# Moving three pieces of work in the first batch of a quantised residual adapter stack, and the rounding of x2 in every batch

## The chip, the cores and the metric

The kernel runs on one core of one Trainium2 chip. The time is the device time of one launch in microseconds (us): 489.69 us, the median of three runs that lay between 489.37 and 489.79. Lower is better. Four engines compute side by side, each with its own program in its own order: TensorE (PE), VectorE (DVE), ScalarE (ACT) and GpSimd (POOL). SyncE (SP) issues the DMAs. They are tied together by semaphores alone.

## The reference, cut to what matters

The input x has 8 batches of 256 tokens of 1024 features. Four residual layers follow each other:

```python
# layer 0: 8 thresholds pick one (delta, zero point) pair for each element
gi  = sum(|x| <= thresholds);  idx = min(gi, 7)
d, zp = deltas[idx], zero_points[idx]
q   = (clip(round(x / d) + zp, 0, 63) - zp) * d
x   = x + where(gi == 8, 0, q)
# layer 1: one 1024x1024 weight per batch, out of 8
x   = x + x @ W1[adapter[b]].T
# layer 2: a shared 1024x1024 weight and a rank-32 adapter
x   = x + x @ W2.T + 0.5 * (x @ lora_A[labeler[b]]) @ lora_B.T
# layer 3: a rank-16 adapter
x   = x + (x @ B3[adapter[b]].T) @ A3[adapter[b]].T
```

All in float32. In the kernel layers 2 and 3 become one product x2 (I + W2)^T and one low-rank product of rank 48: small tables G and E, computed once at the start, fold the adapter of layer 3 over the result of layer 2.

## The kernel before, in words

**Units and steps.** The 256 tokens of a batch are two units of 128 tokens, so there are 16 units. Unit c takes eight steps on ACT and DVE, one for each threshold group; a step is numbered n, and step n belongs to unit n // 8. In step n ACT does `multiple(n)` (L329: x / d plus a rounding constant, into tq) and `exceeds(n-2)` (L344: the mask |x| > threshold), DVE does `value(n)` (L439), `clamp(n-1)` (L448) and `select(n-2)` (L460, a predicated copy under the mask). After the last step of a unit DVE's `close_unit` (L466, L448, L473) writes x1 of that unit; ACT's absx (L337) follows for the next one. ACT and DVE both run this loop written out in full, each with its other duties attached to fixed steps by a table of numbers: with s = n - 16 b, the rounding of x2 (`round_x2` on ACT, L353, to x2h) and its remainder (`split_x2` on DVE, L479, to x2l) stood at s = 13 and 15 for the first unit of a batch and at 21 and 23 for the second one (`X2_AT`), the rounding of the low-rank factor U at 19, 20 (ACT) and 21 (DVE), that of V at 14 and 15.

**PE in one batch.** `w1_x1(b, 0)` is 64 float32 products (128 records, L598) that write x2 of the first unit into two banks of 4 tiles; each bank is released to ACT when its 4 tiles are done. Then `product(0, k)` for k = 0 to 7 (L620): x2h times w2h, x2h times w2l, x2l times w2h, each in two halves of 512 columns; k = 0 to 3 need the first half of x2l, k = 4 to 7 the second. Then PE waits for x1 of the second unit, does `w1_x1(b, 1)`, the low-rank `v_x2` (L611) and `product(1, k)`, and goes over to the next batch. The last low-rank step of batch b (`u_low`, L630 and L632) is done inside `w1_x1(b+1, 0)`, after three tiles.

**The first batch.** It also prepares the tables. PE computes D (`bilinear`, L562) and G (`adapters_g`, L572, L574). ACT copies G out (L394), and SP stores it to DRAM and reads a slice back for each batch. `adapters_e` (L586, L587) makes E into four banks; ACT copies it to outb (L404), SP stores it. W2 comes in eight pieces of 512 KB through four staging buffers, three in `ring` and one in `ua`; POOL adds the identity on the diagonal (L290), ACT rounds a piece (L400, to w2h), DVE takes the remainder (L511, to w2l), and the buffer is free for the piece four further on. `ua` is also where U lands, so U of batch 0 may be loaded only when the last piece that used `ua` is split. Before, ACT did the eight pieces in steps 9 to 16, DVE in steps 10 to 17, one a step; PE waited for w2l of piece k before `product(0, k)`.

SP issues in the order of its program; a wait in it holds all that is behind. In a batch it loads V, x of the second unit of the next batch, the first quarter of W1 of the next batch, then waits until U is split (`ul_ready`), loads U, and then the other three quarters of W1.

Of the kernel before, what the change touches and what calls it, by code (L numbers as in the profile page):

```python
# [5 lines left out]
def quantised_residual_adapter_stack(nc, x, params, w1, w2t, w2n, b3t, b2n, b2r, a3, la, ids_b, ids_a,  # L6
# [13 lines left out]
    B, _, UN, KT, _ = x.shape  # L20
    T = UN * P
    OT = KT
    G = params.shape[2]
# [6 lines left out]
    HALF = KT // 2  # L30
# [15 lines left out]
    with ctx:  # L46
# [47 lines left out]
        stage = [ring[:, i, :] for i in range(ST - 1)] + [ua[:, :]]  # L94
# [78 lines left out]
        def _(sp):  # L173
# [69 lines left out]
            sp.wait_ge(w2l_ready, KT)  # L243
# [64 lines left out]
        DVE_D, ACT_G = 5, 9  # L308
        ACT_E = (15, 15, 16, 16)
        ACT_W2, DVE_W2 = 9, 10  # L310

        X2_AT = (13, 15)

        ACT_V, DVE_V = 14, 15
        ACT_U, DVE_U = 19, 21
# [6 lines left out]
        def _(act):  # L322
# [67 lines left out]
            def tables(n):  # L390
# [6 lines left out]
                if ACT_W2 <= n < ACT_W2 + KT:  # L397
                    k = n - ACT_W2
                    act.wait_ge(w2_diag, k + 1)
                    nc.scalar.activation(w2h[:, k, :], stage[k % ST], ACT.Copy).then_inc(w2h_ready, 1)  # L400
# [8 lines left out]
            for n in range(END):  # L409
# [4 lines left out]
                for i in range(2):  # L414
                    c, off = divmod(n - X2_AT[i], G)
                    if off == 0 and 0 <= c < UN * B:
                        round_x2(c, i)
# [17 lines left out]
        def _(dve):  # L435
# [64 lines left out]
            def tables(n):  # L500
# [7 lines left out]
                if DVE_W2 <= n < DVE_W2 + KT:  # L508
                    k = n - DVE_W2
                    dve.wait_ge(w2h_ready, k + 1)  # L510
                    nc.vector.tensor_tensor(w2l[:, k, :], stage[k % ST], w2h[:, k, :].bitcast(f32),  # L511
                                            ALU.subtract).then_inc(w2l_ready, 1)
# [14 lines left out]
            for n in range(END):  # L527
# [18 lines left out]
                for i in range(2):  # L546
                    c, off = divmod(n - X2_AT[i], G)
                    if off == 0 and 0 <= c < UN * B:
                        split_x2(c, i)
# [7 lines left out]
        def _(pe):  # L557
# [59 lines left out]
            def product(t, k, halves=(0, 1)):  # L617
                for xs, w in ((x2h, w2h), (x2h, w2l), (x2l, w2h)):
# [18 lines left out]
            def batch(b, first=False, last=False):  # L637
                pe.wait_ge(x1_ready, UN * b + 1)
                if first:
                    w1_x1(b, 0, range(OT))  # L640
                    adapters_e()
# [5 lines left out]
                for k in range(KT):  # L647
                    if k % HALF == 0:
                        pe.wait_ge(x2l_ready, BANKS * b + k // HALF + 1)
                    if first:  # L650
                        if k == 0:
                            pe.wait_ge(g_ready, 2)
                        pe.wait_ge(w2l_ready, k + 1)
                    elif k == 0:
                        pe.wait_ge(out_ready, ACCS * (b - 1) + 2)
                    product(0, k)
                pe.wait_ge(x1_ready, UN * b + 2)
                if first:
                    pe.wait_ge(e_ready, 2 * EH)
                w1_x1(b, 1, range(OT))  # L660
# [10 lines left out]
                if last:  # L671
                    for h in range(2):
                        for k in range(early, KT):
                            product(1, k, (h,))
# [9 lines left out]
            adapters_g()  # L684
            batch(0, first=True)
# [53 lines left out]
```

## Time and profile before

| what | value |
|---|---|
| median of three runs | 489.69 us |
| the profiled execution, its own time | 490.88 us |
| its span | 489.1 us |
| PE busy | 467.4 us, 96% of the span |
| DVE busy | 416.3 us, 85% |
| ACT busy | 355.2 us, 73% |

All rows below come from the one profiled execution, whose own time is 1.8 us more than its span. A row of the timeline gives the start (us from the span's start), how long, the engine, the line, the operation, out <- in, the number of instructions, and in brackets how long the engine had been idle before it and what released it. The records of one engine overlap a little (the next one starts before the end of the last is recorded), so the price of an operation in a sequence is best read from start to start. The heavy parts of PE are seen as groups of 128 records of L598, once for each unit.

### The profile page before, as it was taken

What the parts mean: (1) busy time and instruction counts of PE and PEld (TensorE: products, weight loads), DVE (VectorE), ACT (ScalarE), POOL (GpSimd) and SP (SyncE); (2) the same over time, 40 slices, a digit from 0 to 9 for tenths busy, and PEclk for the clock granted to TensorE, in tenths of its full rate; (3) what the DMA queues carried; (4) which work ended last, traced back from release to release, by engine and by line L of the source; (5) the groups of instructions that cost most, each with busy time, mean ns of one, the idle gap of its engine ahead of it and who ended that gap; (6) DMA issues with size and microseconds to landing.
All of it is one profiled execution on the core that took longest, in us unless ns stands there. A gap on an engine that the chain in (4) does not pass through costs nothing.

```text
span 489.1 us, 8214 instructions
## 1 busy us (share of the span) xinstructions
PE 467.4 (96%) x3184; PEld 427.3 (87%) x3184; DVE 416.3 (85%) x480; ACT 355.2 (73%) x384; POOL 52.7 (11%) x46
## 2 busy tenths in 40 slices
PE   3959989999999999999999999999999999999997
PEld 3959669899898979899898979899898979899995
DVE  4999989988999789978999799978999799979310
ACT  6968589759878588759878588759878588758011
POOL 1064100400012001300022000300022001200000
PEclk9998999999999999999999999999999999999999
DMA  7997136612381116512381116512381116502002
GB/s 277 412 373 261 44 119 193 244 44 85 100 325 56 43 59 203 216 43 81 109 306 67 44 59 208 211 43 84 112 302 66 43 60 208 210 2 86 1 1 86
DMA packets 17830, 67.07 MB, mean 137 GB/s; under 512 B 2576, under 2 KB 5904, under 8 KB 13712
## 3 DMA queue, kind: packets, MB, share of 16 engines
q1 hardware_dynamic: 17808, 66.81, 38.1%
q8 instruction: 10, 0.16, 0.1%
q14 instruction: 12, 0.10, 0.1%
HBM read 56.84 MB, written 9.96 MB: 137 GB/s over the span
## 4 chain that ended last, share of the span: by engine, by line
PE 75%; DVE 12%; ACT 9%; issue 2%; DMA 1%; DVEq 0%; SPq 0%; ACTq 0%
PE x_bank L598 48%; PE acc L620 20%; ACT tq L329 4%; DVE y L460 4%; PE x_bank L611 3%; ACT mask L344 3%; DVE uq L466 2%; DVE x L473 2%; PE acc L632 2%; PE acc L630 2%; ACT outb L388 1%; DVE tq L439 1%; DVE y L448 1%; DVE uq L448 1%; DMA xin<-x 1%
## 5 line engine op out<-in xcount | busy, mean ns | idle before, releaser
L598 PEld LDWEIGHTS x_bank<-x,w1b 128*128 128x128 f32 x2048 | 234.2, 194 | 14.8 <-DVE x L473 13.5
L598 PE MATMUL x_bank<-x,w1b 128*128 128x128 f32 x2048 | 235.9, 277 | 10.4 <-DVE x L473 10.4
L329 ACT ACTIVATE tq<-xin,magic,rdelta 128x1024 f32<-128x1024 f32 x128 | 157.1, 1236 | 3.3 <-DMA xin<-x 3.1
L460 DVE COPY_PREDICATED y<-mask,uq 128x1024 f32<-128x1024 int16 x112 | 150.8, 1346 | 0.1
L344 ACT ACTIVATE mask<-absx,negtop 128x1024 bf16<-128x1024 f32 x112 | 127.8, 1141 | 6.2 <-DVE y L460 5.7
L439 DVE TENSOR_SCALAR tq<-tq,par 128x1024 f32<-128x1024 f32 x128 | 98.4, 769 | 11.6 <-ACT tq L329 5.4
L448 DVE TENSOR_SCALAR uq<-tq,ylow,yhigh 128x1024 f32<-128x1024 f32 x112 | 91.8, 820 | 3.3 <-issue 1.7
L295 POOL TENSOR_TENSOR w1b<-w1b,eye 128x256 f32<-128x256 f32 x32 | 42.0, 1312 | 364.5 <-DMA w1b<-w 364.5
L620 PE MATMUL acc<-w2h,x2h 128*128 128x512 f32 x256 | 81.1, 394 | 0.0
L620 PE MATMUL acc<-w2l,x2h 128*128 128x512 f32 x256 | 80.1, 390 | 0.0
L620 PE MATMUL acc<-w2h,x2l 128*128 128x512 f32 x256 | 79.9, 389 | 0.0
L353 ACT ACTIVATE x2h<-x_bank 128x512 fp32r<-128x512 f32 x32 | 19.1, 597 | 80.8 <-PE x_bank L598 80.8
L620 PEld LDWEIGHTS acc<-w2l,x2h 128*128 128x128 f32 x256 | 48.1, 188 | 10.2
L620 PEld LDWEIGHTS acc<-w2h,x2l 128*128 128x128 f32 x256 | 48.1, 188 | 10.2
L479 DVE TENSOR_TENSOR x2l<-x_bank,x2h 128x512 fp32r<-128x512 f32 x32 | 22.0, 689 | 37.8 <-ACT x2h L353 37.0
L620 PEld LDWEIGHTS acc<-w2h,x2h 128*128 128x128 f32 x256 | 46.5, 188 | 8.8 <-DVE x2l L479 0.2
L337 ACT ACTIVATE absx<-xin 128x1024 f32<-128x1024 f32 x16 | 16.9, 1056 | 9.3 <-DVE uq L466 9.3
L388 ACT ACTIVATE outb<-acc 128x512 f32<-128x512 f32 x32 | 18.0, 593 | 7.5 <-PE acc L632 7.5
L466 DVE SCALAR_TENSOR_TENSOR uq<-absx,top,y 128x1024 f32<-128x1024 f32 x16 | 22.9, 1432 | 0.6
L473 DVE TENSOR_TENSOR x<-xin,uq 128x1024 f32<-128x1024 f32 x16 | 20.0, 1252 | 0.0
L574 PE MATMUL acc<-x,w1b 128*128 128x128 f32 x128 | 18.0, 301 | 0.0
L574 PEld LDWEIGHTS acc<-x,w1b 128*128 128x128 f32 x128 | 17.4, 218 | 0.0
(56 smaller groups left out, 217.1 us busy)
## 6 DMA issues: line engine op xcount, KB each, us to landing
w1b<-w SPq DMA_DIRECT2D x32, 1024.0 KB, 6.5
xin<-x SPq DMA_DIRECT2D x16, 512.0 KB, 3.7
out<-outb SPq DMA_DIRECT2D x14, 512.0 KB, 2.7
w1b<-w2n SPq DMA_DIRECT2D x4, 1024.0 KB, 10.1
ring<-w2t SPq DMA_DIRECT2D x6, 512.0 KB, 7.3
ua<-e_dram SPq DMA_DIRECT2D x16, 128.0 KB, 2.5
ua<-w2t SPq DMA_DIRECT2D x2, 512.0 KB, 6.1
va<-la SPq DMA_DIRECT2D x8, 128.0 KB, 2.7
```

Of the source, the lines that this page charges most:

```text
L295: nc.gpsimd.tensor_tensor(diag, diag, eye[:, :].unsqueeze(1).to_broadcast([P, 2, P]), ALU.add) \
L329: nc.scalar.activation(tq[:, n % TQ, :], flat(xin, c % UN), ACT.Identity, bias=magic[:, 0:1], scale=rdelta[:, g:g + 1]).then_inc(t_ready, 1)
L344: nc.scalar.activation(mask[:, n % MK, :], absx[:, :], ACT.Relu, bias=negtop[:, g:g + 1], scale=1.0).then_inc(mask_ready, 1)
L388: nc.scalar.activation(outb[:, t, h * DH:(h + 1) * DH], acc[q][:, :], ACT.Copy).then_inc(out_ready, 1)
L439: nc.vector.tensor_scalar(tq[:, n % TQ, :], tq[:, n % TQ, :], -MAGIC, par[:, 1, g:g + 1], ALU.add, ALU.mult).then_inc(u_ready, 1)
L448: nc.vector.tensor_scalar(clamped_y, tq[:, n % TQ, :], ylow[:, g:g + 1], yhigh[:, g:g + 1], ALU.max, ALU.min).then_inc(clamped, 1)
L460: nc.vector.copy_predicated(y[:, :], mask[:, n % MK, :].bitcast(i16), uq[:, n % 2, :]) \
L466: nc.vector.scalar_tensor_tensor(ycut, absx[:, :], top[:, G - 1:G], y[:, :], ALU.is_gt, ALU.mult).then_inc(y_cut, 1)
L473: nc.vector.tensor_tensor(flat(x1, c % UN), flat(xin, c % UN), ycut, ALU.add).then_inc(x1_ready, 1)
L574: last = nc.tensor.matmul(into, w2g[:, i, o * P:(o + 1) * P], b3s[:, o, :], start=False, stop=(o == OT - 1))
L598: last = nc.tensor.matmul(x2_bank[2 * t + i][:, o % HALF * P:(o % HALF + 1) * P], w1b[:, o, at:at + P], x1[:, t, k, :], start=(o % HALF == ...
L620: nc.tensor.matmul(acc[2 * t + h][:, :], xs[:, t, k, :], w[:, k, h * DH:(h + 1) * DH], start=(k == 0 and xs is x2h and w is w2h), stop=Fal ...
```

## The change

1. `adapters_e` is called behind `adapters_g`, ahead of the first batch, and no longer between `w1_x1(0, 0)` and the first product. ACT's copies of E go from steps 15, 15, 16, 16 to 12, 13, 13, 14.
2. ACT rounds x2 at s = 14 and 16 (and 22 and 24), a step further on than before; DVE's remainder stays at 13 and 15 (21 and 23). ACT and DVE run in step only through their semaphores, so ACT may be ahead of DVE by a step or more.
3. In the first batch the product of the first unit is cut: the two parts with w2h for all eight k, then the part with w2l for k = 0 to 3, then `w1_x1(0, 1)`, and then the part with w2l for k = 4 to 7. PE waits for w2h of a piece at the first, for w2l at the second and third. DVE splits pieces 0 to 3 in steps 10 to 13 as before, and pieces 4 to 7 in steps 18 to 21.
4. The four staging buffers are renamed: `ua` holds pieces 0 and 4 in place of 3 and 7, and SP loads U of batch 0 when five pieces are split instead of eight.
5. The rounding of U is two steps later in every batch (ACT 21 and 22, DVE 23), ACT's copy of G one step later (10).

```diff
-        stage = [ring[:, i, :] for i in range(ST - 1)] + [ua[:, :]]
+        stage = [ua[:, :]] + [ring[:, i, :] for i in range(ST - 1)]
...
-            sp.wait_ge(w2l_ready, KT)
+            sp.wait_ge(w2l_ready, ST + 1)
             load_u(a0)
...
-        DVE_D, ACT_G = 5, 9
-        ACT_E = (15, 15, 16, 16)
-        ACT_W2, DVE_W2 = 9, 10
-
-        X2_AT = (13, 15)
+        DVE_D, ACT_G = 5, 10
+        ACT_E = (12, 13, 13, 14)
+        ACT_W2, DVE_W2 = (9, 10, 11, 12, 13, 14, 15, 16), (10, 11, 12, 13, 18, 19, 20, 21)
+
+        ACT_X2, DVE_X2 = (14, 16), (13, 15)
...
-        ACT_U, DVE_U = 19, 21
+        ACT_U, DVE_U = 21, 23
...
-            def product(t, k, halves=(0, 1)):
-                for xs, w in ((x2h, w2h), (x2h, w2l), (x2l, w2h)):
+            HIGH, LOW = ((x2h, w2h), (x2l, w2h)), ((x2h, w2l),)
+            ALL = (HIGH[0], LOW[0], HIGH[1])
+
+            def product(t, k, parts=ALL, halves=(0, 1)):
+                for xs, w in parts:
...
                 if first:
                     w1_x1(b, 0, range(OT))
-                    adapters_e()
...
-                        pe.wait_ge(w2l_ready, k + 1)
+                        pe.wait_ge(w2h_ready, k + 1)
...
-                    product(0, k)
+                    product(0, k, HIGH if first else ALL)
+                if first:
+                    for k in range(HALF):
+                        pe.wait_ge(w2l_ready, k + 1)
+                        product(0, k, LOW)
+                    pe.wait_ge(e_ready, 2 * EH)
                 pe.wait_ge(x1_ready, UN * b + 2)
+                w1_x1(b, 1, range(OT))
                 if first:
-                    pe.wait_ge(e_ready, 2 * EH)
-                w1_x1(b, 1, range(OT))
+                    for k in range(HALF, KT):
+                        pe.wait_ge(w2l_ready, k + 1)
+                        product(0, k, LOW)
...
             bilinear()
             adapters_g()
+            adapters_e()
             batch(0, first=True)
```

**PE, the start of the first batch.** acc and x2_bank are the banks of PSUM, outb holds the inputs of E. Before:

```order
L574 MATMUL acc1<-x1,w1b 128x128 x8
L598 MATMUL x2_bank0<-x1,w1b 128x128 x32
L598 MATMUL x2_bank1<-x1,w1b 128x128 x32
L586 MATMUL acc2<-outb,eye 128x512
L587 MATMUL acc2<-outb,dmask 128x512
L586 MATMUL acc3<-outb,eye 128x512
L587 MATMUL acc3<-outb,dmask 128x512
L586 MATMUL x2_bank2<-outb,eye 128x512
L587 MATMUL x2_bank2<-outb,dmask 128x512
L586 MATMUL x2_bank3<-outb,eye 128x512
L587 MATMUL x2_bank3<-outb,dmask 128x512
L620 MATMUL acc0<-w2h,x2h 128x512
```

The same place in the changed kernel:

```order
L574 MATMUL acc1<-x1,w1b 128x128 x8
L586 MATMUL acc2<-outb,eye 128x512
L587 MATMUL acc2<-outb,dmask 128x512
L586 MATMUL acc3<-outb,eye 128x512
L587 MATMUL acc3<-outb,dmask 128x512
L586 MATMUL x2_bank2<-outb,eye 128x512
L587 MATMUL x2_bank2<-outb,dmask 128x512
L586 MATMUL x2_bank3<-outb,eye 128x512
L587 MATMUL x2_bank3<-outb,dmask 128x512
L598 MATMUL x2_bank0<-x1,w1b 128x128 x32
L598 MATMUL x2_bank1<-x1,w1b 128x128 x32
L623 MATMUL acc0<-w2h,x2h 128x512
```

The eight products of E moved from behind the W1 product to ahead of it; the line of the W2 product is L623 in the changed kernel.

**DVE, the first batch, from the second remainder of x2 to x1 of the second unit.** L479 is the remainder of x2, L511 that of a piece of W2, L473 writes x1. Before:

```order
L479 TENSOR_TENSOR x2l<-x_bank,x2h 128x512
L460 COPY_PREDICATED y<-mask,uq 128x1024
L511 TENSOR_TENSOR w2l<-ring,w2h 128x1024
L439 TENSOR_SCALAR tq<-tq,par 128x1024
L448 TENSOR_SCALAR uq<-tq,ylow,yhigh 128x1024
L460 COPY_PREDICATED y<-mask,uq 128x1024
L511 TENSOR_TENSOR w2l<-ua,w2h 128x1024
L439 TENSOR_SCALAR tq<-tq,par 128x1024
L460 COPY_PREDICATED y<-mask,uq 128x1024
L466 SCALAR_TENSOR_TENSOR uq<-absx,top,y 128x1024
L448 TENSOR_SCALAR y<-tq,ylow,yhigh 128x1024
L473 TENSOR_TENSOR x<-xin,uq 128x1024
```

The same stretch in the changed kernel:

```order
L479 TENSOR_TENSOR x2l<-x_bank,x2h 128x512
L460 COPY_PREDICATED y<-mask,uq 128x1024
L439 TENSOR_SCALAR tq<-tq,par 128x1024
L448 TENSOR_SCALAR uq<-tq,ylow,yhigh 128x1024
L460 COPY_PREDICATED y<-mask,uq 128x1024
L439 TENSOR_SCALAR tq<-tq,par 128x1024
L460 COPY_PREDICATED y<-mask,uq 128x1024
L466 SCALAR_TENSOR_TENSOR uq<-absx,top,y 128x1024
L448 TENSOR_SCALAR y<-tq,ylow,yhigh 128x1024
L473 TENSOR_TENSOR x<-xin,uq 128x1024
L511 TENSOR_TENSOR w2l<-ua,w2h 128x1024
```

The remainders of W2 left this stretch and stand behind L473 (two more left the stretch just before it).

**ACT, a later batch, around the rounding of x2 of the first unit.** L353 is the rounding, from x2_bank0 and x2_bank1; L388 copies the result of the batch before. Before:

```order
L344 ACTIVATE mask<-absx,negtop 128x1024
L353 ACTIVATE x2h<-x2_bank0 128x512
L329 ACTIVATE tq<-xin,magic,rdelta 128x1024
L344 ACTIVATE mask<-absx,negtop 128x1024
L388 ACTIVATE outb<-acc0 128x512
L388 ACTIVATE outb<-acc1 128x512
L362 ACTIVATE v_hl<-va 128x8x32
L363 ACTIVATE v_hl<-vg 128x8x16
L329 ACTIVATE tq<-xin,magic,rdelta 128x1024
L344 ACTIVATE mask<-absx,negtop 128x1024
L353 ACTIVATE x2h<-x2_bank1 128x512
L388 ACTIVATE outb<-acc2 128x512
```

The same place in the changed kernel:

```order
L344 ACTIVATE mask<-absx,negtop 128x1024
L353 ACTIVATE x2h<-x2_bank0 128x512
L388 ACTIVATE outb<-acc0 128x512
L388 ACTIVATE outb<-acc1 128x512
L362 ACTIVATE v_hl<-va 128x8x32
L363 ACTIVATE v_hl<-vg 128x8x16
L329 ACTIVATE tq<-xin,magic,rdelta 128x1024
L344 ACTIVATE mask<-absx,negtop 128x1024
L388 ACTIVATE outb<-acc2 128x512
L329 ACTIVATE tq<-xin,magic,rdelta 128x1024
L344 ACTIVATE mask<-absx,negtop 128x1024
L353 ACTIVATE x2h<-x2_bank1 128x512
```

Each rounding now has one more pair of L329 and L344 ahead of it and one fewer behind it.

## Rows read from the trace of the kernel before

**Rows 1.** The page, part 1: busy time of each engine (share of the span), instructions.

```profile
PE 467.4 (96%) x3184; PEld 427.3 (87%) x3184; DVE 416.3 (85%) x480; ACT 355.2 (73%) x384; POOL 52.7 (11%) x46
```

**Rows 2.** Waits of PE: who waited for whom, us in total, times, longest.

```profile
PE x_bank L598 <- DVE x L473: 10.4, 8, 5.0
```

**Rows 3.** Timeline of PE, first batch.

```profile
35.64 17.21 PE L598 MATMUL x_bank<-x,w1b 128*128 128x128 f32 x128 [5.02 <-DVE x L473]
52.69 1.02 PE L586 MATMUL acc<-outb,eye 128*128 128x512 f32 x2
...
72.60 14.56 PE L598 MATMUL x_bank<-x,w1b 128*128 128x128 f32 x128 [1.95 <-DVE x L473]
...
99.79 5.52 PE L598 MATMUL x_bank<-x,w1b 128*128 128x128 f32 x48
```

**Rows 4.** Windows of PE: stretch, length, busy (count), granted clock, DMA share, GB/s.

```profile
34.00:35.00 1.00, 0.00 (x0) 0.71 1.08 352
```

**Rows 5.** Timeline of PE, later batches.

```profile
181.69 0.61 PE L620 MATMUL acc<-w2h,x2l 128*128 128x512 f32 x2
182.80 14.56 PE L598 MATMUL x_bank<-x,w1b 128*128 128x128 f32 x128 [0.50 <-DVE x L473]
...
209.99 5.52 PE L598 MATMUL x_bank<-x,w1b 128*128 128x128 f32 x48
...
456.78 14.45 PE L598 MATMUL x_bank<-x,w1b 128*128 128x128 f32 x128
```

**Rows 6.** Timeline of DVE, the second and third batch.

```profile
122.50 0.75 DVE L439 TENSOR_SCALAR tq<-tq,par 128x1024 f32<-128x1024 f32 x1 [0.91 <-ACT mask L344]
...
172.06 0.69 DVE L479 TENSOR_TENSOR x2l<-x_bank,x2h 128x512 fp32r<-128x512 f32 x1 [0.47 <-ACT x2h L353]
...
174.77 0.81 DVE L448 TENSOR_SCALAR uq<-tq,ylow,yhigh 128x1024 f32<-128x1024 f32 x1
...
177.42 0.75 DVE L439 TENSOR_SCALAR tq<-tq,par 128x1024 f32<-128x1024 f32 x1 [0.56 <-ACT mask L344]
...
181.53 1.22 DVE L473 TENSOR_TENSOR x<-xin,uq 128x1024 f32<-128x1024 f32 x1
...
192.07 0.68 DVE L479 TENSOR_TENSOR x2l<-x_bank,x2h 128x512 fp32r<-128x512 f32 x1
...
202.82 0.91 DVE L439 TENSOR_SCALAR tq<-tq,par 128x1024 f32<-128x1024 f32 x1 [0.20 <-DVE y L460]
...
207.43 1.22 DVE L473 TENSOR_TENSOR x<-xin,uq 128x1024 f32<-128x1024 f32 x1
```

**Rows 7.** Timeline of ACT, the third batch.

```profile
164.28 0.60 ACT L353 ACTIVATE x2h<-x_bank 128x512 fp32r<-128x512 f32 x1 [4.98 <-PE x_bank L598]
164.77 1.23 ACT L329 ACTIVATE tq<-xin,magic,rdelta 128x1024 f32<-128x1024 f32 x1
165.91 1.14 ACT L344 ACTIVATE mask<-absx,negtop 128x1024 bf16<-128x1024 f32 x1
...
171.43 0.60 ACT L353 ACTIVATE x2h<-x_bank 128x512 fp32r<-128x512 f32 x1 [0.74 <-PE x_bank L598]
...
190.25 0.60 ACT L353 ACTIVATE x2h<-x_bank 128x512 fp32r<-128x512 f32 x1 [0.96 <-PE x_bank L598]
```

**Rows 8.** Timeline of DVE, first batch.

```profile
51.32 1.20 DVE L511 TENSOR_TENSOR w2l<-ring,w2h 128x1024 fp32r<-128x1024 f32 x1
...
58.27 0.68 DVE L479 TENSOR_TENSOR x2l<-x_bank,x2h 128x512 fp32r<-128x512 f32 x1
...
71.32 1.22 DVE L473 TENSOR_TENSOR x<-xin,uq 128x1024 f32<-128x1024 f32 x1
...
97.94 1.22 DVE L473 TENSOR_TENSOR x<-xin,uq 128x1024 f32<-128x1024 f32 x1
```

**Rows 9.** Timeline of ACT, first batch.

```profile
41.04 1.04 ACT L400 ACTIVATE w2h<-ua 128x1024 fp32r<-128x1024 f32 x1
```

**Rows 10.** The page, part 6: DMA issues, KB each, us from issue to landing.

```profile
w1b<-w SPq DMA_DIRECT2D x32, 1024.0 KB, 6.5
```

More of the change, by code:

```diff
@@ L396, in tables @@
                                              ACT.Copy).then_inc(g_ready, 1)
-                if ACT_W2 <= n < ACT_W2 + KT:
-                    k = n - ACT_W2
+                if n in ACT_W2:
+                    k = ACT_W2.index(n)
                     act.wait_ge(w2_diag, k + 1)
@@ L414, in _ @@
                 for i in range(2):
-                    c, off = divmod(n - X2_AT[i], G)
+                    c, off = divmod(n - ACT_X2[i], G)
                     if off == 0 and 0 <= c < UN * B:
@@ L507, in tables @@
                         .then_inc(dmask_ready, 1)
-                if DVE_W2 <= n < DVE_W2 + KT:
-                    k = n - DVE_W2
+                if n in DVE_W2:
+                    k = DVE_W2.index(n)
                     dve.wait_ge(w2h_ready, k + 1)
@@ L546, in _ @@
                 for i in range(2):
-                    c, off = divmod(n - X2_AT[i], G)
+                    c, off = divmod(n - DVE_X2[i], G)
                     if off == 0 and 0 <= c < UN * B:
@@ L673, in batch @@
                         for k in range(early, KT):
-                            product(1, k, (h,))
+                            product(1, k, ALL, (h,))
                         if h == 0:
```

## The prediction, made before the changed kernel ran

> **What bounds the kernel now.** The page comes first: PE is busy for 96% of the span [rows 1]. So the time is PE's work plus the little that PE waits. The waits of PE are the second view: nearly all that belongs to the batches is one kind, the W1 product waits for x1 from DVE, eight times, 10.4 us [rows 2]. PE's timeline splits the sum: 5.02 and 1.95 us in the first batch [rows 3], five waits of 0.50 in the third to seventh [rows 5], which leaves 0.9 for the second; the last batch has none. A W1 product behind a wait is recorded with 14.56 us, the one that did not wait (at 456.78) with 14.45, so a wait also costs a start-up of 0.11 [rows 5].
>
> Two more costs are in these rows. The first W1 product took 17.21 us instead of 14.56 [rows 3], because PE had stood still for 5.02 us and the granted clock had fallen from 2.4 towards 1.2 GHz near 34.5 us [rows 4]: 2.65 us. And PE's wait for the x1 of a second unit is DVE's chain from the second remainder of x2 to L473. In the third batch DVE is held twice there by ACT: L439 idles 0.56 us for a mask at 177.42, and L448 at 174.77 starts some 0.2 late for the mask before it [rows 6].
>
> **The steady part: rounding a step later.** ACT idles 4.98 us before it rounds the first bank of x2 [rows 7], waiting for PE, and only afterwards does the L329 and L344 that DVE will want. With the rounding behind them that pair (1.14 + 1.03 = 2.17 us, the second being 1.14 less an overlap of 0.1 [rows 7]) falls into the idle time. ACT from 164.28 is then: rounding 0.49, two result copies 0.97, V 0.5, pair 2.17, a result copy 0.49, pair 2.17, which is 171.07. PE gives the second bank for rounding at 171.43 [rows 7]. So ACT gets there 0.36 us early, the second rounding is not late, and DVE's L479 stays at 172.06 [rows 6]. The copy and V prices are estimates from the 0.49 of an equal or larger tile.
>
> Behind it ACT needs 0.49 + 0.49 + 2.17 for the mask that held DVE: 174.6, or about 175.1 if the mask waits for the predicated copy two steps back. DVE wants it at about 176.9. Both holds go. What stays of the 0.56 is 0.20, the time DVE needs for its own copy's signal at a unit's end, as at 202.82 [rows 6]. DVE gains 0.36 + 0.20 = 0.56 per batch. PE's gap is from the last product, 181.69 + 0.45 = 182.14, to 182.80, that is 0.66 [rows 5], so 0.10 of it stays and the start-up too. Five batches: 5 x 0.56 = 2.8. In the second batch the hold was 0.91 [rows 6]: 0.71 + 0.20 = 0.91, of a PE gap of about 1.05. Sum of the steady part 3.7 us.
>
> The bounds of this term: nothing, if DVE remains held; 5 x (0.66 + 0.11) + 1.05 + 0.11 = 5.0 us if PE never waits again. I take 3.7 since each piece of it is in a row.
>
> **What the later step costs elsewhere.** For a second unit DVE's first remainder was not held: 192.07, no idle [rows 6]. ACT rounded at 190.25, after a wait of 0.96 for PE [rows 7]. Now a pair of 2.17 and one more U rounding order stand ahead; U itself (two pieces of 0.95) has moved back, so ACT reaches the rounding at about 190.25 - 0.96 - 0.95 + 2.17 + some waiting for DVE's copy = 190.5 to 191.0. It ends near 191.5. DVE no longer has the 1.25 us of the U remainder ahead and arrives at 192.07 - 1.25 = 190.8. It waits 0.7 to 0.8, ends up 0.5 us ahead of before, and then pays the U remainder two steps on: 0.7 late. x1 of the next first unit was ready at 207.43 + 1.22 = 208.65, and PE wanted it at 209.99 [rows 5, 6]: slack 1.34, of which 0.7 is used. Cost nothing. SP holds three quarters of W1 until U is split, now some 6.6 us later (two steps of 2.6 and a remainder). They land 6.5 us after the issue [rows 10], near 206 to 210; PE wants the second quarter two tiles (3.6 us) behind 209.99. Cost nothing, and 3 us later it would begin to cost.
>
> **The first batch.** E is eight times 0.86 us (1.02 recorded for a pair of records, 0.16 of it overlap [rows 3]): 6.9. It stood between 52.8 and 59.7, on PE's path. G ends at 35.64 - 5.02 = 30.6. E fills 30.6 to 37.5, in the old wait, and the clock has no reason to fall. The W1 product starts 1.9 later, at 37.5, and takes 14.5: it ends at 52.0 instead of 52.8. PE is then 7.7 us earlier at the W2 product. That gain can't pass: PE next needs x1 of the second unit, which comes from DVE.
>
> DVE is the same up to its first remainder of x2 near 49.5. ACT sets the second: piece 3 of W2 is rounded at 41.04, when POOL gives it [rows 9], and until the second rounding of x2 stand four W2 pieces (4 x 0.95 = 3.8; 1.04 recorded less overlap), four pairs (8.7), four copies of E and the first rounding (5 x 0.49 = 2.45), V 0.5 and about 0.3 for POOL's next diagonal: 15.7, so it starts at 56.7. DVE's second remainder follows 0.63 later, as 172.06 follows 171.43 [rows 6, 7]: 57.3 instead of 58.27 [rows 8]. From there to L473 it is now exactly the sequence of a later batch, whose 181.53 - 172.06 = 9.47 less the 0.56 held gives 8.91: L473 starts at 66.2 instead of 71.32 [rows 8], 5.1 us sooner. Two pieces of W2 and 1.9 us of being held left this stretch. x1 is ready at 67.45 and PE, which has waited since about 63.5 (a part of the W2 product also waits, near 55.6 to 58), starts `w1_x1(0, 1)` at 67.5 and not at 72.60.
>
> PE then works as before, 99.79 - 72.60 = 27.19 us, plus the eight products with w2l that were put behind (4 x 0.45 = 1.8). It is done at 96.5. But DVE pays for the four W2 pieces now: from L473 to the next L473 26.62 us before, and 4 x 1.13 more (1.20 less overlap [rows 8]) is 31.1. The next L473 starts at 97.3, x1 is ready at 98.55, PE starts at 98.6. Before it was 99.79 without a wait. The gain is 99.79 - 98.6 - 0.11 = 1.1 us. **That is what remains of the 5.1:** PE waits 2.1 us in a new place. Bounds: nothing, if DVE loses one more microsecond on this path; 99.79 - 96.5 = 3.3 if it loses none to the four pieces.
>
> **Sum.** 1.1 + 3.7 = 4.8. The profiled execution had 490.88, so 486.1 for its like; the median of the runs stands 1.19 lower, and I apply the difference to it: 489.69 - 4.8 = 484.9 us.
>
> **The rivals.**
> A. The clock falls in the new wait. PE stands still from 63.5 to 67.5, 4.0 us. 1.95 us did not lower the clock (the product behind it took 14.56), 5.02 did [rows 3], at about 3.9 us from its start [rows 4]. Price: the next W1 product 2.65 longer, PE done at 99.1 instead of 96.5, x1 long there at 98.6. The slack of 2.1 hides most of it: 0.5 us, so 485.4.
> The Trainium skill, in TensorE: Matmul & The Clock Gate, under HAM oscillation, warns that a pause of PE between bursts can put the clock at half so that the next burst starts slow. By that rule this rival would be the likely case; the trace agrees for 5.02 us and shows the contrary for 1.95.
>
> B. The steady part gives nothing: DVE is held by something else in the same stretch (its own signals, ACT late after all since the early margin is only 0.36). For it: PE's gap of 0.66 is small and DVE is busy 85% [rows 1]. Against it: both holds name the mask. 489.69 - 1.1 = 488.6.
>
> C. Slower. x1 of the first unit of each next batch comes late, because DVE's first remainder of a second unit now waits for an ACT that runs a further step ahead. Its slack is 1.34, I use 0.7. If ACT arrives one more pair late (2.17), PE waits 2.17 - 0.64 + 0.11 = 1.6 in six transitions: 9.8 us lost, 489.69 - 4.8 + 9.8 = 494.7. It turns slower than before when ACT is more than 1.4 us later than worked out. Against it: ACT idled 0.96 there [rows 7], and its busy share is 73% [rows 1].
>
> D. DVE's chain gains more than I count, and PE never waits in the steady part and hardly at 98.6: 489.69 - 5.0 - 2.2 = 482.5.
>
> **Chances.** My forecast 0.55, A 0.18, B 0.12, C 0.06, D 0.09. The likeliest one's own range is 484.2 to 485.8. The range of 8 in 10 takes in A and most of D and goes part of the way to B: 483.0 to 487.4. A measurement of this kernel tells 0.2%, about 1 us, from no change. B sits on that line, half of it counts as the same. Faster 0.88, same 0.06, slower 0.06.
>
> **What would show it.** E stands at 30.6 to 37.5 and the granted clock stays at 2.4 GHz up to 52. x1 of the second unit near 67.4, and PE waits about 4 us for it, then about 2 us for the next one near 98.6. In later batches L439 at a second unit's end is released by DVE's own copy after 0.20, and PE's waits fall from 0.50 to 0.1 or less. ACT's second rounding still idles for PE. It would be wrong if DVE's L479 waited more than 1 us for the rounding of a second unit, if the waits of 0.50 stayed, or if PE waited for W1's second quarter.

## The result, and the profile after

The changed kernel took 486.01 us (median of 5 runs, 484.91 to 486.41) where the kernel before took 489.69 (489.16 to 490.94). The ratio is 0.9919 with the interval 0.9903 to 0.9935: 3.7 us faster, forecast 4.8 (484.9, range 483.0 to 487.4). The profiled execution had 486.40 us and a span of 484.6, so 4.48 less than its counterpart before. The rows below place all of this 4.48. The medians differ by only 3.68: the profiled execution of the kernel before was 1.19 us above its median, that of the changed kernel 0.39 above its own. So 0.80 of the 4.48 lies in which executions were profiled, and the rows can't say where in the kernel before.

The page, part 1, of the changed kernel. It answers to [rows 1].

```profile
PE 465.8 (96%) x3184; PEld 426.1 (88%) x3184; DVE 418.6 (86%) x480; ACT 359.5 (74%) x384; POOL 45.2 (9%) x46
```

PE's work is the same within 0.4%, and PE is still the bound. Waits of the changed kernel, the lines on PE and two on ACT: who waited for whom, us in total, times, longest. The first line, ahead of the rest, is from the kernel before.

```profile
ACT mask L344 <- DVE y L460: 5.7, 9, 0.8
```

```profile
ACT mask L344 <- DVE y L460: 40.1, 48, 2.5
...
ACT x2h L353 <- PE x_bank L598: 28.7, 16, 13.4
...
PE x_bank L598 <- DVE x L473: 4.0, 2, 3.7
...
PE acc L623 <- DVE x2l L479: 3.3, 1, 3.3
```

The 10.4 us in eight waits for x1 [rows 2] are 4.0 in two, and one wait for the second remainder of x2 is new. ACT now waits for DVE's copies before its masks, 40.1 us where it was 5.7: it has run ahead, which is what removes DVE's holds. Timeline of PE, changed kernel, the answer to [rows 3, 5]:

```profile
29.45 1.02 PE L586 MATMUL acc<-outb,eye 128*128 128x512 f32 x2
...
36.31 14.45 PE L598 MATMUL x_bank<-x,w1b 128*128 128x128 f32 x128
...
57.68 0.73 PE L623 MATMUL acc<-w2h,x2h 128*128 128x512 f32 x2 [3.27 <-DVE x2l L479]
...
61.44 1.98 PE L623 MATMUL acc<-w2l,x2h 128*128 128x512 f32 x8
67.16 17.30 PE L598 MATMUL x_bank<-x,w1b 128*128 128x128 f32 x128 [3.75 <-DVE x L473]
84.22 2.09 PE L623 MATMUL acc<-w2l,x2h 128*128 128x512 f32 x8
...
98.96 5.52 PE L598 MATMUL x_bank<-x,w1b 128*128 128x128 f32 x48
...
126.46 14.56 PE L598 MATMUL x_bank<-x,w1b 128*128 128x128 f32 x128 [0.28 <-DVE x L473]
153.65 5.52 PE L598 MATMUL x_bank<-x,w1b 128*128 128x128 f32 x48
...
180.26 0.61 PE L623 MATMUL acc<-w2h,x2l 128*128 128x512 f32 x2
180.74 14.56 PE L598 MATMUL x_bank<-x,w1b 128*128 128x128 f32 x128
...
207.96 5.52 PE L598 MATMUL x_bank<-x,w1b 128*128 128x128 f32 x48
...
425.24 5.52 PE L598 MATMUL x_bank<-x,w1b 128*128 128x128 f32 x48
```

Three things are to be seen. E stands at 29.45, in the old wait, and the first W1 product has its full speed. The second W1 product starts 5.4 us earlier than before, yet takes 17.30 us, and the second batch (98.96, before 99.79) starts only **0.83 us** earlier. From there to the last batch's first product are 425.24 - 98.96 = 326.28 us, before 429.72 - 99.79 = 329.93: **3.65 us** less in six periods. 0.83 + 3.65 = 4.48, the whole difference of the spans.

Windows of PE, changed kernel (columns as in [rows 4]):

```profile
66.00:67.00 1.00, 0.00 (x0) 0.58 0.00 0
...
72.00:73.00 1.00, 1.00 (x6) 0.51 0.00 0
73.00:74.00 1.00, 1.00 (x11) 1.00 0.00 0
```

The granted clock fell from 2.4 to 1.2 GHz near 66.2, while PE stood still for x1, and came back at 73.0. Six products in a microsecond become eleven: the same work at half the clock. Timeline of DVE, changed kernel, the answer to [rows 6, 8]:

```profile
56.93 0.69 DVE L479 TENSOR_TENSOR x2l<-x_bank,x2h 128x512 fp32r<-128x512 f32 x1 [0.52 <-ACT x2h L353]
...
65.80 1.22 DVE L473 TENSOR_TENSOR x<-xin,uq 128x1024 f32<-128x1024 f32 x1
...
96.52 1.21 DVE L473 TENSOR_TENSOR x<-xin,uq 128x1024 f32<-128x1024 f32 x1
...
121.11 0.75 DVE L439 TENSOR_SCALAR tq<-tq,par 128x1024 f32<-128x1024 f32 x1 [0.57 <-DVE y L460]
...
170.62 0.69 DVE L479 TENSOR_TENSOR x2l<-x_bank,x2h 128x512 fp32r<-128x512 f32 x1 [0.71 <-ACT x2h L353]
...
175.41 0.75 DVE L439 TENSOR_SCALAR tq<-tq,par 128x1024 f32<-128x1024 f32 x1 [0.20 <-DVE y L460]
...
179.47 1.22 DVE L473 TENSOR_TENSOR x<-xin,uq 128x1024 f32<-128x1024 f32 x1
...
189.52 0.69 DVE L479 TENSOR_TENSOR x2l<-x_bank,x2h 128x512 fp32r<-128x512 f32 x1 [0.86 <-ACT x2h L353]
...
206.19 1.21 DVE L473 TENSOR_TENSOR x<-xin,uq 128x1024 f32<-128x1024 f32 x1
```

In the third batch L439 is held 0.20 by DVE's own copy, and no longer 0.56 by ACT's mask. In the second batch 0.57 of the 0.91 stays. Timeline of ACT, changed kernel, the answer to [rows 7]:

```profile
56.31 0.59 ACT L353 ACTIVATE x2h<-x_bank 128x512 fp32r<-128x512 f32 x1
...
162.84 0.60 ACT L353 ACTIVATE x2h<-x_bank 128x512 fp32r<-128x512 f32 x1 [0.93 <-PE x_bank L598]
...
169.99 0.60 ACT L353 ACTIVATE x2h<-x_bank 128x512 fp32r<-128x512 f32 x1 [0.25 <-PE x_bank L598]
```

The wait of 4.98 before the first rounding is 0.93. The pair of L329 and L344 (2.17) fills about half of the difference; most of the rest has turned into waits for DVE's copies ahead of the masks (0.64 us before, 1.56 + 0.36 now, between 150 us and the rounding). The second rounding still idles 0.25 for PE, so it is not late.

### The profile page after: what moved, and what is told of

Read it like the earlier page. It is cut to its first block, busy times and chain, and to the rows that moved or that the text cites. A ratio compares the mean times of both kernels' runs of the same rounds, so it can differ in the third digit from the quotient of the medians.

```text
span 484.6 us, 8214 instructions
## 1 busy us (share of the span) xinstructions
PE 465.8 (96%) x3184; PEld 426.1 (88%) x3184; DVE 418.6 (86%) x480; ACT 359.5 (74%) x384; POOL 45.2 (9%) x46
## 4 chain that ended last, share of the span: by engine, by line
PE 83%; DVE 8%; ACT 4%; DMA 2%; issue 1%; POOL 0%; DVEq 0%; SPq 0%; ACTq 0%
PE x_bank L598 45%; PE acc L623 32%; DVE y L460 4%; PE x_bank L611 3%; PE acc L635 2%; PE acc L633 2%; DVE uq L448 1%; ACT tq L329 1%; DMA ua<-w2t 1%; DMA xin<-x 1%; DVE x L473 1%; DVE uq L466 1%; ACT mask L344 1%; DVE tq L439 1%; ACT w2h L400 1%
## 5 line engine op out<-in xcount | busy, mean ns | idle before, releaser
L329 ACT ACTIVATE tq<-xin,magic,rdelta 128x1024 f32<-128x1024 f32 x128 | 157.0, 1234 | 3.7 <-DMA xin<-x 3.4
L344 ACT ACTIVATE mask<-absx,negtop 128x1024 bf16<-128x1024 f32 x112 | 128.5, 1147 | 40.8 <-DVE y L460 40.1
L439 DVE TENSOR_SCALAR tq<-tq,par 128x1024 f32<-128x1024 f32 x128 | 98.5, 769 | 8.5 <-ACT tq L329 4.8
L623 PE MATMUL acc<-w2h,x2h 128*128 128x512 f32 x256 | 80.9, 393 | 3.3 <-DVE x2l L479 3.3
L623 PE MATMUL acc<-w2h,x2l 128*128 128x512 f32 x256 | 79.9, 389 | 0.0
L623 PE MATMUL acc<-w2l,x2h 128*128 128x512 f32 x256 | 79.1, 390 | 0.0
L295 POOL TENSOR_TENSOR w1b<-w1b,eye 128x256 f32<-128x256 f32 x32 | 34.6, 1083 | 370.9 <-DMA w1b<-w 370.9
L623 PEld LDWEIGHTS acc<-w2h,x2l 128*128 128x128 f32 x256 | 48.1, 188 | 10.2
L623 PEld LDWEIGHTS acc<-w2l,x2h 128*128 128x128 f32 x256 | 48.0, 188 | 10.2
L623 PEld LDWEIGHTS acc<-w2h,x2h 128*128 128x128 f32 x256 | 46.3, 188 | 11.9 <-DVE x2l L479 3.7
L479 DVE TENSOR_TENSOR x2l<-x_bank,x2h 128x512 fp32r<-128x512 f32 x32 | 22.1, 689 | 36.2 <-ACT x2h L353 36.2
L353 ACT ACTIVATE x2h<-x_bank 128x512 fp32r<-128x512 f32 x32 | 19.0, 592 | 29.1 <-PE x_bank L598 28.7
L388 ACT ACTIVATE outb<-acc 128x512 f32<-128x512 f32 x32 | 18.1, 598 | 7.5 <-PE acc L635 7.5
L473 DVE TENSOR_TENSOR x<-xin,uq 128x1024 f32<-128x1024 f32 x16 | 20.0, 1249 | 0.0
L574 PE MATMUL acc<-x,w1b 128*128 128x128 f32 x128 | 16.9, 289 | 0.0
L611 PE MATMUL x_bank<-x2h,v_hl 128*128 128x256 f32 x64 | 16.3, 290 | 0.0
```

The costliest lines, as they stand in the source:

```text
L295: nc.gpsimd.tensor_tensor(diag, diag, eye[:, :].unsqueeze(1).to_broadcast([P, 2, P]), ALU.add) \
L329: nc.scalar.activation(tq[:, n % TQ, :], flat(xin, c % UN), ACT.Identity, bias=magic[:, 0:1], scale=rdelta[:, g:g + 1]).then_inc(t_ready, 1)
L344: nc.scalar.activation(mask[:, n % MK, :], absx[:, :], ACT.Relu, bias=negtop[:, g:g + 1], scale=1.0).then_inc(mask_ready, 1)
L439: nc.vector.tensor_scalar(tq[:, n % TQ, :], tq[:, n % TQ, :], -MAGIC, par[:, 1, g:g + 1], ALU.add, ALU.mult).then_inc(u_ready, 1)
L473: nc.vector.tensor_tensor(flat(x1, c % UN), flat(xin, c % UN), ycut, ALU.add).then_inc(x1_ready, 1)
L479: nc.vector.tensor_tensor(x2l[:, t, tiles, :].rearrange("p k t -> p (k t)"), x2_bank[2 * t + i][:, :], x2h[:, t, tiles, :].rearrange("p k ...
```

## The experiments

Two profile figures are given for most kernels: **start** is the start of the second batch's first W1 product (before 99.79, changed 98.96), **six** is the time from it to the last batch's (before 329.93, changed 326.28). The kernel before ran beside each: median 489.88 us beside the first four, 490.41 beside the next four, 489.46 beside the last four. One profile has one start, and starts of one kernel can differ by a microsecond or two, in part since W2's pieces come at other times; a claim on the first batch therefore wants a median as well.

**Only the rounding a step later**, on the kernel before.

```diff
-        X2_AT = (13, 15)
+        ACT_X2, DVE_X2 = (14, 16), (13, 15)
```

> The kernel before with ACT's rounding of x2 at 14 and 16 and nothing else. Main theory (ACT held DVE through the masks): the first batch is as before (W1 product of the second batch starts near 99.8 us), the periods between first units fall from 54.93 to about 54.3 and in the second batch from 55.30 to 54.7: 489.7 - 3.6 = 486.1 us. Rival (the steady gain of the changed kernel needs U two steps later too, because U ahead of the rounding of the second unit holds DVE): x1 of first units late, periods 54.6 or more, 487.5 or more.

Measured: 491.09 us, ratio 1.0029 (1.0015 to 1.0043), slower. six 326.38: the steady gain is whole. start 102.98: the first batch lost 3.2 us, which I had not expected. Timeline of ACT, this kernel:

```profile
58.53 1.09 ACT L404 ACTIVATE outb<-acc 128x512 f32<-128x512 f32 x2 [5.42 <-PE x_bank L587]
...
61.67 0.59 ACT L353 ACTIVATE x2h<-x_bank 128x512 fp32r<-128x512 f32 x1
```

ACT's copies of E stand in step 15. The second rounding, moved to 16, is now behind them, and PE has E done only at 58.5. DVE waits 4.38 us for it (L479 at 62.30), and x1 comes at 73.13 + 1.22. The other part is the clock. PE in this kernel:

```profile
74.41 15.92 PE L598 MATMUL x_bank<-x,w1b 128*128 128x128 f32 x128 [3.55 <-DVE x L473]
```

x1 is 1.81 later than before (L473 at 71.32 there), and behind the longer wait (3.55 for 1.95) the W1 product takes 1.36 more: 1.81 + 1.36 = 3.17 of the 3.19. So the later rounding wants E's copies out of its way.

**The rounding and U's later step**, on the kernel before.

```diff
-        X2_AT = (13, 15)
+        ACT_X2, DVE_X2 = (14, 16), (13, 15)
-        ACT_U, DVE_U = 19, 21
+        ACT_U, DVE_U = 21, 23
```

> As the one before, and U two steps later on ACT and DVE (21 and 22, 23). Main theory: the steady part of the changed kernel whole, 486.1 us, periods 54.3 as there. Rival (U matters): 1 us or more faster than the kernel with the rounding alone. Second rival (three quarters of W1 later cost something): slower than the rounding alone.

Measured: 491.19 us, 1.0025 (1.0009 to 1.0042); six 326.48, start 103.93. Against the run before it U's step is worth nothing in the steady part.

**Only the first batch's part**: the changed kernel with rounding and U on their old steps.

```diff
-        ACT_X2, DVE_X2 = (14, 16), (13, 15)
+        ACT_X2, DVE_X2 = (13, 15), (13, 15)
-        ACT_U, DVE_U = 21, 23
+        ACT_U, DVE_U = 19, 21
```

> The changed kernel with the rounding of x2 back at 13 and 15 and U back at 19 and 21: E behind G, the cut of the W2 product and the staging remain. Main theory: periods as before the change (54.93, 55.30), the W1 product of the second batch near 98.9 where the clock falls in PE's wait in the first batch and near 97.9 where it does not: 488.9 or 487.9 us. Rival (the rounding a step later is what makes the first batch quicker): the W1 product of the second batch starts at 99.8 or later, 489.7.

Measured: 490.94 us, 1.0011 (0.9994 to 1.0028). six 330.04 shows that the steady gain is the rounding's alone. start 100.77, where a gain was expected. Timeline of ACT, this kernel:

```profile
74.14 1.06 ACT L370 ACTIVATE u_hh<-ua 128x1024 fp32r<-128x1024 f32 x1 [5.56 <-DMA ua<-a]
```

The `ua` tile now holds W2's fifth piece, so SP loads U only when DVE has taken that remainder, behind L473: it starts at 68.21 here, the loads of U go out from 69.6 on, and ACT wants U in step 19, at 68.6. U's later step is thus not idle: it covers this load. The last experiment tests that. This profile is of one of the longer executions (491.97; they lie between 488.54 and 492.12), and W2's fifth piece held ACT 2.41 us in it.

**E behind G alone**, on the kernel before.

```diff
-        ACT_E = (15, 15, 16, 16)
+        ACT_E = (12, 13, 13, 14)
...
-                    adapters_e()
...
+            adapters_e()
```

> The kernel before with E behind G and ACT's copies of E at 12, 13, 13, 14, nothing else. DVE keeps four remainders of W2 ahead of x1 of the second unit; ACT no longer stands still for E. Main theory: DVE loses its 1.7 us of being held there, x1 of the second unit ready near 70.8 instead of 72.5; PE waits for it about 4 us, so the clock may fall: start of the second batch's W1 product 98.0 with the clock kept (488.0 us), 100.7 with the clock lost (490.6 us). Rival (moving E gives PE its 7 us back): 484 or less.

Measured: 489.61 us, 0.9998 (0.9986 to 1.001): nothing. Timeline of PE, this kernel:

```profile
37.52 14.45 PE L598 MATMUL x_bank<-x,w1b 128*128 128x128 f32 x128
...
70.11 17.05 PE L598 MATMUL x_bank<-x,w1b 128*128 128x128 f32 x128 [3.54 <-DVE x L473]
...
99.81 5.52 PE L598 MATMUL x_bank<-x,w1b 128*128 128x128 f32 x48
```

E took 6.9 us off PE's path, and none of it reached 99.8: PE waits for x1, the clock falls in that wait, and the W1 product gives back 2.5 (17.05 for 14.56), just what its earlier start had won (70.11 for 72.60). In one of the twelve executions the mean granted clock was 1.00: that one took 488.41 us, the shortest of all, and the one with the lowest clock (0.989) 491.58.

**The changed kernel without the cut of the W2 product.**

```diff
-        ACT_W2, DVE_W2 = (9, 10, 11, 12, 13, 14, 15, 16), (10, 11, 12, 13, 18, 19, 20, 21)
+        ACT_W2, DVE_W2 = (9, 10, 11, 12, 13, 14, 15, 16), (10, 11, 12, 13, 14, 15, 16, 17)
...
-                    product(0, k, HIGH if first else ALL)
+                    product(0, k)
-                if first:
-                    for k in range(HALF):
-                        pe.wait_ge(w2l_ready, k + 1)
-                        product(0, k, LOW)
...
-                if first:
-                    for k in range(HALF, KT):
-                        pe.wait_ge(w2l_ready, k + 1)
-                        product(0, k, LOW)
```

> The changed kernel with the W2 product of the first unit whole again and DVE's remainders of W2 in steps 10 to 17, one a step; E, staging, rounding and U as changed. Main theory: DVE meets all eight remainders ahead of x1 of the second unit, as before, which is ready near 71 us; the same work is only moved from behind L473 to ahead of it, so x1 of the next batch's first unit is ready at the same time, near 98, and PE, which then has less to do between, is ready at about 71 + 27.2 = 98.2 with the clock kept and 100.9 with it lost. So the cut is worth 0 to 2 us in the first batch: 485 to 488 us. Rival (the cut is what makes the first batch quicker): 3 us or more slower than the changed kernel.

Measured: 486.88 us, 0.9936 (0.9912 to 0.996); six 326.41, start 99.34. L473 is at 69.16 and the next at 97.37, where the changed kernel has 65.80 and 96.52. The cut brings x1 3.4 us forward and the next x1 0.85, and 0.4 at the start of the second batch. The W1 product between them took 16.16 here and 17.30 there, so part of what the cut brings goes to the clock. The interval overlaps the changed kernel's: in time, the cut's gain is not shown.

**Twelve more products before the wait for x1** (their result is overwritten), to hold the clock.

```diff
+                    for _ in range(12):
+                        nc.tensor.matmul(acc[2][:, :], x2h[:, 0, 0, :], w2h[:, 0, 0:DH], start=True, stop=False,
+                                         skip_group_check=True)
```

> The changed kernel with 12 idle products of 512 columns (2.7 us) into a free bank of the second unit at the start of PE's wait for x1 of the second unit; their results are overwritten. Main theory (the clock fell in that wait and made the W1 product 17.3 us instead of 14.5): clock at 1.00 all through, product 14.5 us, PE ready 2.8 us sooner for the second batch, but x1 of its first unit comes at 97.7, so only 1.1 us of it arrive: 1.1 us faster than the changed kernel where the clock had fallen (486.4 to 485.3), nothing where it had not. Rival (the product was long for another reason, DMA or POOL): no change. Rival (the clock's cost was whole on the path): 2.7 us faster, 483.7.

Measured: 484.90 us, 0.9895 (0.9871 to 0.992). six 326.55. Timeline and windows of PE, this kernel:

```profile
57.60 1.03 PE L623 MATMUL acc<-w2h,x2h 128*128 128x512 f32 x2 [2.45 <-DVE x2l L479]
...
64.76 2.88 PE L665 MATMUL acc<-w2h,x2h 128*128 128x512 f32 x12
67.48 14.45 PE L598 MATMUL x_bank<-x,w1b 128*128 128x128 f32 x128
...
97.77 5.62 PE L598 MATMUL x_bank<-x,w1b 128*128 128x128 f32 x48 [1.20 <-DVE x L473]
```

```profile
57.00:58.00 1.00, 0.40 (x2) 0.92 0.00 0
58.00:59.00 1.00, 1.00 (x4) 0.50 0.00 0
...
61.00:62.00 1.00, 1.00 (x5) 0.87 0.00 0
```

The W1 product is back at 14.45, and now PE waits for x1 at 97.77. Of the 2.85 saved 1.2 arrive, the rest is hidden by that x1. This second wait is the one that I had forecast. But the clock did not hold all through, as I had expected: in this execution it fell at 57.8, behind a pause of only 2.45 us, and came back at 61.3. The W2 product ended later for it, and the wait that the twelve products filled was about 2.2 us and not 3.75. The profile alone therefore does not show that they kept the clock. Better evidence are the six executions: their mean granted clock is 1.00 once and 0.999 twice (484.75, 484.86 and 484.92 us), and in none of the eleven executions of the changed kernel is it above 0.996. The interval of the ratio overlaps the changed kernel's.

**DVE's second remainder a step later too.**

```diff
-        ACT_X2, DVE_X2 = (14, 16), (13, 15)
+        ACT_X2, DVE_X2 = (14, 16), (13, 16)
```

> The changed kernel with DVE's second remainder of x2 a step later (16 in place of 15), so that DVE doesn't wait 0.71 us for the bank that PE has just finished. Main theory (in the steady part what is left of PE's wait is DVE's chain from that bank): x1 of second units 0.7 us sooner, PE's remaining wait with its start-up, 0.1 to 0.2 us a batch, goes: 1.0 us faster. Rival (PE alone sets the steady part now): the same within 0.2 us. Rival (PE needs x2l of the fifth tile sooner than it then comes): slower by 1 us or more.

Measured: **483.35 us** (482.57 to 483.48), 0.9854 (0.9827 to 0.9882), faster than both kernels. start 97.24, six 325.12. Timelines of PE and then of DVE, and windows of PE, this kernel:

```profile
59.48 1.12 PE L623 MATMUL acc<-w2h,x2h 128*128 128x512 f32 x2 [5.05 <-DVE x2l L479]
...
66.64 14.45 PE L598 MATMUL x_bank<-x,w1b 128*128 128x128 f32 x128
...
97.24 5.62 PE L598 MATMUL x_bank<-x,w1b 128*128 128x128 f32 x48 [1.08 <-DVE x L473]
...
178.59 14.45 PE L598 MATMUL x_bank<-x,w1b 128*128 128x128 f32 x128
```

```profile
170.29 0.71 DVE L479 TENSOR_TENSOR x2l<-x_bank,x2h 128x512 fp32r<-128x512 f32 x1
...
176.57 1.22 DVE L473 TENSOR_TENSOR x<-xin,uq 128x1024 f32<-128x1024 f32 x1
```

```profile
59.00:60.00 1.00, 0.52 (x2) 0.81 0.00 0
60.00:61.00 1.00, 1.00 (x4) 0.50 0.00 0
...
63.00:64.00 1.00, 1.00 (x6) 0.98 0.00 0
```

Two gains. In the steady part DVE no longer idles 0.71 for the rounding at this place, x1 is ready at 176.57 + 1.22 = 177.79, 0.80 before PE wants it, and the start-up of 0.11 has gone (14.45): 1.16 in six periods. In the first batch the two waits of 3.27 and 3.75 have become one of 5.05, ahead of the W2 product. The clock falls behind it for 3.4 us (59.6 to 63.0), and is back before the W1 product, whose x1 is then there.

**Both of these together.**

```diff
-        ACT_X2, DVE_X2 = (14, 16), (13, 15)
+        ACT_X2, DVE_X2 = (14, 16), (13, 16)
...
+                    for _ in range(12):
```

> The idle products and the later remainder together. Main theory: both are worth their own and more, since the later remainder brings both x1 of the first batch sooner: 1.1 + 1.0 + 0.5 = 2.5 us faster than a run of the changed kernel with the clock lost: 483.8. Rival (one of the two does not hold): as the better of the two alone.

Measured: 485.14 us, 0.9901 (0.9874 to 0.9928). The intervals overlap by a little, but all six executions (483.92 to 486.47) are slower than all five of the later remainder alone (482.57 to 483.48). six 324.99, start 98.58. Timeline of PE, this kernel:

```profile
66.92 2.88 PE L665 MATMUL acc<-w2h,x2h 128*128 128x512 f32 x12
69.64 14.45 PE L598 MATMUL x_bank<-x,w1b 128*128 128x128 f32 x128
```

The clock had fallen at 57.6, in a pause of 3.46, and stayed low until 64.4, twice as long as in the kernel with the later remainder alone. So the W2 product ended only at about 66.9. x1 was ready at 64.10 + 1.22 = 65.32, so there was no wait left to fill, and the twelve products, 2.7 us, stood on the path. My expectation that the two add is refuted.

**The changed kernel again**, as a control beside the next three.

> The changed kernel once more, as the control of this call: 485 to 486.4 us. The first batch ends in one of two ways: with the clock fallen in PE's wait for x1 of the second unit (W1 product near 17 us, the second batch's near 98.9) or kept (14.5 and 97.8), 1.1 us apart.

Measured: 485.84 us, 0.9923 (0.9898 to 0.9948). Its W1 product, at 66.86, took 17.42, behind a wait of 3.72: the lower clock is not one execution's accident. start 98.76, six 326.49.

**The later remainder, with the first four w2l tiles taken before the second half.**

```diff
-        ACT_X2, DVE_X2 = (14, 16), (13, 15)
+        ACT_X2, DVE_X2 = (14, 16), (13, 16)
...
+                    if first and k == HALF:
+                        for j in range(HALF):
+                            pe.wait_ge(w2l_ready, j + 1)
+                            product(0, j, LOW)
...
-                    for k in range(HALF):
-                        pe.wait_ge(w2l_ready, k + 1)
-                        product(0, k, LOW)
```

> The changed kernel with DVE's second remainder of x2 at 16, and in the first batch the w2l part of k = 0 to 3 ahead of the w2h parts of k = 4 to 7, so that PE's pause for x2l (5.1 us with the later remainder) is 1.8 shorter. Main theory: what decides is DVE, x1 of the next first unit near 97.2, and PE is there sooner either way; so the same as with the later remainder alone, 483.4 us, with the clock kept more often. Rival (PE's pauses in the first batch still cost): 1 us or more faster than that, 482.4.

Measured: 483.36 us (482.41 to 485.48), 0.9863 (0.9843 to 0.9883): the same as without it, and 2.5 below the control. The pause ahead of the W2 product splits (1.13 and 3.24), but its end is DVE's. "The clock kept more often" did not come: no execution has a mean clock above 0.996, and behind the pause of 3.24 it was low from 60.8 to 67.6. The profile is of the slowest execution (485.48), in which W2's fifth piece held ACT 3.23 us: start 99.26, six 325.10.

**The rounding alone once more, with E's copies behind it.**

```diff
-        ACT_E = (15, 15, 16, 16)
+        ACT_E = (16, 16, 17, 17)
-        X2_AT = (13, 15)
+        ACT_X2, DVE_X2 = (14, 16), (13, 15)
```

> The kernel before with the rounding at 14 and 16 and ACT's copies of E at 16, 16, 17, 17; E stays behind the W1 product on PE. Main theory (with the rounding alone the first batch lost 3.2 us because the second rounding stood behind ACT's wait for E): the second rounding comes near 56 us, x1 of the second unit near 71, the second batch's W1 product at 98 to 99.5, periods 54.3: 484.5 to 486. Rival (the loss had another cause, so that E must be behind G for the rounding to pay): 489 or more.

Measured: 487.26 us, 0.9953 (0.9938 to 0.9968), so 3.8 below the 491.09 of the first experiment. The second rounding is at 57.73 instead of 61.67, with no wait ahead of it; six 326.26. So the first experiment's loss came from that wait. start is 100.43, 2.55 sooner than there, as L473 is 2.72 sooner (70.41). The size was off (I expected at most 486): the W1 product at 71.68 again took 16.11, with a low clock, and that takes back more than the 0.91 by which x1 is sooner than in the kernel before.

**The changed kernel with the old rounding, U's later step kept.**

```diff
-        ACT_X2, DVE_X2 = (14, 16), (13, 15)
+        ACT_X2, DVE_X2 = (13, 15), (13, 15)
```

> The changed kernel with only the rounding of x2 back at 13 and 15; U stays at 21 and 22, 23. With U back as well ACT stood 5.6 us for U's load. Main theory (U had to move since the load of U now waits for a remainder that comes behind x1): ACT does not stand for U, the second batch's W1 product starts at 97.9 to 99.2, periods 54.9: 488 to 489 us. Rival (U is not the cause): 490.5 or more, as with U at 19.

Measured: 488.43 us, 0.9979 (0.9965 to 0.9993); start 96.30, six 330.13. So it was U's load that cost the third experiment its gain: 1.0011 against 0.9979 (their intervals just miss each other, 0.9994 and 0.9993), some 1.6 us. The profiles agree: from L473 to the next L473 DVE takes 32.33 us there and 30.87 here, 1.46 more. The wait of 5.56 is thus not its price. It also shows a cost that I had not forecast. The second rounding of the first batch is here at 52.41, in the changed kernel at 56.31, and L473 at 64.08 instead of 65.80. The later rounding gives 330.13 - 326.28 = 3.85 in the steady part, and by the medians beside each other (488.43 and the control's 485.84) only 2.59 in all: it takes some 1.3 us back in the first batch (in the profiles the next L473 1.57 and start 2.66, of which 1.14 is the clock: the W1 product took 16.16 here and 17.30 in the changed kernel).

## Why the prediction was right, and where it was not

**The steady part: right.** Forecast 3.7, measured 3.65; with the rounding alone 3.55 and 3.67, without it none (329.90 to 330.13 in three kernels, 329.93 before). The step by step account holds as well. DVE from L479 to L473 took 179.47 - 170.62 = 8.85, forecast 8.91. The hold that stays is 0.20. At a second unit L479 waits 0.86, forecast 0.7 to 0.8, and x1 of the next first unit is ready at 207.40, 0.56 before PE's 207.96, forecast 0.64 of slack. Two terms were mis-sized and cancel: a later batch gained 0.61 and not 0.56 (five: 3.04 and not 2.8), and the second batch 0.61 and not 0.91, since 0.57 and not 0.20 of its hold stays at 121.11. The step that failed there is "0.71 + 0.20", which gave all but 0.20 of the hold of 0.91 to ACT's mask. The trace before already spoke against it: its later batches have 0.56 at this place, 0.35 less, and in the changed kernel the second batch again has 0.37 more than the later ones (0.57 and 0.20). So some 0.36 us of the second batch's hold was most likely never ACT's. The same 0.57 stands in the kernel with the rounding alone, in the one with E's copies behind it and in the one with the later remainder. What it is stays open; no experiment was aimed at it.

**The first batch: near in the two profiles, by two errors that cancel, and less by the medians.** Forecast 1.1, in the two profiles 0.83. The medians differ by 489.69 - 486.01 = 3.68, beside the control by 489.46 - 485.84 = 3.62, and that is the steady part alone. By the interval of the ratio the whole is 3.2 to 4.7 us, which leaves nothing to 1.1 us for the first batch. So the total, forecast at 4.8, came out about 1 us lower, and it is this term that is short. What follows explains the profiled pair. E's place, the first W1 product's full speed and PE's wait near 63.5 to 67.2 came as worked out. The second rounding came at 56.31 (forecast 56.7), L473 at 65.80 (66.2), the next 30.72 later (31.1): x1 was ready at 97.73, 0.8 sooner than my 98.55. Against that the step "PE is done at 96.5" failed. The clock fell in the wait of 3.75, the W1 product took 17.30 instead of 14.56, and PE was done at 98.96. This is rival A, to which I had given 0.18 and for the forecast with the clock kept 0.55. The two profiles show the fall at this place, and the mean granted clock of all eleven executions of the changed kernel is 0.993 or 0.996: none kept the full clock throughout. Without it PE would have been done at 96.2 and started at about 97.8, as in the profile with the twelve extra products (97.77), and the first batch would have given 1.9. So the clock cost 1.1 to 1.2, not the 0.5 of the rival, because the x1 behind which it hides came sooner.

My reason against A was a row: 1.95 us of standing still had not lowered the clock, and 5.02 had, at 3.9 us from its start (3.8 by the window of 34 to 35 us). I took one such time for a fixed one and 4.0 as just at its edge. The fall came 2.7 us after PE's last product here, and in the experiments between 2.0 and 5.2 us after it: two rows could not carry that step. The Trainium skill, in TensorE: Matmul & The Clock Gate, under HAM oscillation, has pauses between bursts put the clock at half. The trace agrees with its 3.75 us, and does not with its 3.27 us, behind which the clock stayed.

**What I left out.** That the later rounding depends on E's copies having moved (3.2 us without it), that U's later step covers a load (a wait of 5.56 us on ACT and some 1.6 us of time without it), and that the first batch pays for the later rounding. The first two change nothing of the sum here, since all the parts were together.

Rivals B and D fell: six is 3.65 less, not 0 or 5.0. C fell: PE's two waits for x1 are both for a second unit's (67.16, 126.46), none for a first's.

## What to carry to other kernels

A step that moves in an in-order engine's program moves behind everything there, waits included: look in the trace for the longest wait between its old place and its new one before counting the gain. Cover found on one engine (E's 6.9 us) is worth only what the engine that binds next allows; work out that engine's chain to the same point before anything is added up. And if a change makes TensorE wait at a new place, ask what follows the pause. Work with another wait behind it can take the low clock at little cost, since that wait absorbs it; work that leads straight to the next wanted result gives back up to three microseconds here.

## What the runs showed of the hardware

- The length of a pause of PE did not decide alone whether the clock fell. It stayed at 2.4 GHz behind pauses of 3.27 us (changed kernel), 3.12 (the same kernel again) and 2.24 (without the cut), and fell behind single pauses of 2.09 (only the first batch's part) and 2.45 (twelve more products), in both when PE had just started again. One of 3.24 (the w2l tiles taken earlier) had the fall too, and so had all the longer ones, from 3.39 us up.
- Nor is the time from PE's last product to the fall fixed: 2.0 us with E behind G alone, 2.7 in the changed kernel, 3.8 in the kernel before, 4.4 with the old rounding and U's later step kept, 5.2 with the later remainder.
- The low level lasted from 66.2 to 73.0 in the changed kernel, 6.8 us, and from 59.6 to 63.0 in the one with the later remainder, 3.4 us. It cost the W1 product 2.74 us in the first; in the second it fell on W2 products, behind which PE would have waited for x1 anyway until 64.94 + 1.22 = 66.16, and the W1 product started at 66.64.
- One piece of W2 came up to 3 us later in some executions than in others. ACT waited 3.23, 3.02 and 2.41 us for the fifth piece in the profiles of three kernels, and 0.27 in that of the changed one. Whether its load or POOL's addition was late I did not separate.
